# Graph attention with layer norm on one core: the mean for rows without neighbours moved from a VectorE pass into the bias of ScalarE's copy of the outputs

## The reference, cut to what matters

```python
def _L0_gnn_ref(feat_in, adj, W, b, w_src, w_dst, H_w, H_b):
    h = jnp.einsum('bnd,ade->bane', feat_in, W)
    th = jnp.tanh(h)
    attn_src = jnp.einsum('bane,aeo->bano', th, w_src)
    attn_dst = jnp.einsum('bane,aeo->bano', th, w_dst)
    attn = attn_src + jnp.swapaxes(attn_dst, 2, 3)
    attn = jnp.where(attn >= 0, attn, LEAKY_ALPHA * attn)
    mask = ~adj[:, None, :, :]
    attn = jnp.where(mask, jnp.float32(-999.0), attn)
    attn = jax.nn.softmax(attn, axis=-1)
    feat_out = jnp.einsum('banm,bame->bane', attn, h) + b
    feat_out = jnp.swapaxes(feat_out, 1, 2).reshape(feat_in.shape[0], feat_in.shape[1], -1)
    feat_out = jax.nn.elu(feat_out)
    gate = jax.nn.sigmoid(feat_in @ H_w.T + H_b)
    return gate * feat_out + (1.0 - gate) * feat_in
x = _layernorm(x + _L0_gnn_ref(...), axis=-1)
```

## Time and profile before

| | |
|---|---|
| median of 3 runs | 711.69 us (711.6 to 712.4) |
| the profiled execution | 711.58 us, span 709.8 us from first to last instruction |
| busy, share of the span | PE 96%, DVE 96%, POOL 85%, ACT 58% |
| granted TensorE clock, mean | 0.990 of full speed |
| length of one of steps 2 to 13 | 42.0 us |
| busy in 340.00 to 382.00 us | PE 41.46, DVE 41.02, POOL 38.38, ACT 25.56 |

### The profile page before, as it was taken

One profiled execution on the slowest core, in us unless ns is written; L12 is line 12 of the kernel. 1 busy time (PEld: TensorE's weight loads), 2 busy tenths in 40 slices (PEclk: granted clock), 3 DMA queues, 4 the chain that ended last, 5 costly groups with the idle time before them and its releaser, 6 DMA issues.

```text
span 709.8 us, 12409 instructions
## 1 busy us (share of the span) xinstructions
PE 678.0 (96%) x3327; PEld 376.1 (53%) x3327; DVE 678.3 (96%) x1225; ACT 412.4 (58%) x859; POOL 601.0 (85%) x434
## 2 busy tenths in 40 slices
PE   8899999999999999999999999999999999999882
PEld 5464655546555555555655554564646455554530
DVE  7699999999999999999999999999999999999996
ACT  5324558284664838567383765828476482855673
POOL 2964798998989899898989989899898989988393
PEclk9999999999999999999999999999999999999997
DMA  5253335263352615335261443426244351533402
GB/s 193 101 176 117 101 104 196 66 210 112 130 168 94 203 59 188 112 132 173 94 221 59 148 149 134 163 89 213 84 134 163 111 186 61 169 108 128 161 30 89
DMA packets 47083, 94.55 MB, mean 133 GB/s; under 512 B 2962, under 2 KB 28308, under 8 KB 47060
## 3 DMA queue, kind: packets, MB, share of 16 engines
q1 hardware_dynamic: 38868, 82.08, 35.5%
q10 hardware_dynamic: 8192, 12.19, 4.6%
HBM read 81.28 MB, written 12.98 MB: 133 GB/s over the span
## 4 chain that ended last, share of the span: by engine, by line
PE 72%; ACT 10%; DVE 7%; issue 5%; POOL 4%; DMA 2%; ACTq 0%; DVEq 0%; SPq 0%; POOLq 0%
PE out_T L976 37%; PE hg L898 28%; PE tr L984 4%; DVE ew L743 4%; ACT xT_hi L450 3%; ACT scratch L521 2%; ACT att_T L497 1%; PE hg L959 1%; ACT h_sb L462 1%; DMA xT_in<-in_xT 1%; DMA v_all<-v_rows 1%; DVE ex L778 1%; DVE att L761 1%; PE hg L931 1%; DVE att L772 1%
## 5 line engine op out<-in xcount | busy, mean ns | idle before, releaser
L743 DVE SCALAR_TENSOR_TENSOR ew<-v_all,u,adj 128x512 f32<-128x512 f32 x768 | 526.0, 732 | 0.5 <-DMA v_all<-v_rows 0.5
L976 PE MATMUL out_T<-ew,vals 128*64 128x512 f32 x1536 | 367.6, 602 | 2.7 <-DVE ew L743 2.7
L976 PEld LDWEIGHTS out_T<-ew,vals 128*64 128x64 f32 x1536 | 107.3, 137 | 198.3 <-issue 154.7
L301 POOL TENSOR_TENSOR th_w<-th,score_w 128x768 f32<-128x768 f32 x58 | 107.6, 1855 | 48.0 <-ACT th L458 40.8
L497 ACT ACTIVATE att_T<-out_T,tiny 128x512 f32<-128x512 f32 x96 | 65.8, 685 | 134.7 <-PE out_T L976 134.7
L898 PE MATMUL hg<-w_hi,xT_hi 128*128 128x384 f32 x384 | 99.4, 367 | 8.9 <-ACT h_sb L462 6.5
L898 PEld LDWEIGHTS hg<-w_hi,xT_hi 128*128 128x128 f32 x384 | 61.8, 191 | 50.6 <-issue 47.3
L898 PE MATMUL hg<-w_lo,xT_hi 128*128 128x384 f32 x384 | 88.6, 338 | 0.0
L898 PE MATMUL hg<-w_hi,xT_lo 128*128 128x384 f32 x384 | 87.6, 335 | 0.0
L305 POOL TENSOR_TENSOR th_w<-th_w 128x384 f32<-128x384 f32 x58 | 78.1, 1347 | 4.5
L468 ACT ACTIVATE gate_tanh<-hg 128x384 f32<-128x384 f32 x64 | 31.2, 490 | 78.3 <-PE hg L898 78.3
(11 more groups left out here) (106 smaller groups left out, 734.5 us busy)
## 6 DMA issues: line engine op xcount, KB each, us to landing
v_all<-v_rows SPq DMA_DIRECT2D x96, 512.0 KB, 3.8
xT_in<-in_xT SPq DMA_DIRECT2D x16, 768.0 KB, 4.6
x_in<-in_x SPq DMA_DIRECT2D x15, 768.0 KB, 4.5
out<-y ACTq DMA_DIRECT2D x15, 768.0 KB, 5.3
adj_in<-in_adjT SPq DMA_DIRECT2D x16, 256.0 KB, 4.9
xT_in<-in_x SPq DMA_DIRECT2D x1, 768.0 KB, 6.0
ew<-in_W SPq DMA_DIRECT2D x1, 576.0 KB, 4.2
gate<-in_HwT SPq DMA_DIRECT2D x1, 576.0 KB, 8.0
```

Of the source, the lines that this page charges most:

```text
L301: g.tensor_tensor(th_w[:, c % 2], th[:, c].unsqueeze(1).broadcast_to([P, 2, D]), score_w[:], ALU.mult).then_inc(S["thw_done"], 1)
L743: ve.scalar_tensor_tensor(out=ew[:, (2 * C * j + i) % SLOTS, :], in0=v_all[:, j % VSLOTS, k], scalar=u[:, q, c, h:h + 1], in1=ADJ[c][:], o ...
L976: te.matmul(OUT[VW * k:VW * k + VW, :], vals[:, q, c, h, :], ew[:, t % SLOTS, :], start=(c == 0), stop=(c == C - 1)).then_inc(S["ew_free"], 1)
```

## The change

The mean is added before the division. With `TINY` = 2^-90, `mean_w` holds TINY/512, so `means` gives TINY x mean; ScalarE copies it to the new tile `out_bias` (128 x 6, one column for each pair of heads, with TINY itself in the rows of the denominators), and `copy_out(b, j)` adds column j as its `bias`. A row without neighbours then has TINY x mean over TINY. For the other rows to stay exact, `vals` is lifted by 2^60.

- `means` is now three matmuls with `hb_tot` as weights and one column each, into columns 384 to 386 of `HG[1]`. It stands before `attend(b, 0)` in every step.
- `out_biases` on ScalarE: 4 activations of 32 partitions x 3 elements, right before `copy_out(b, 0)`, which waits for them.
- `exps` has one more activation of 128 x 48 and two more waits on ScalarE's own results.
- `alone`, `add_means`, `means_alone` and the additions in the last step are gone. In the last step `exp_late` of the middle columns moves before `copy_out(b, 5)`, and VectorE multiplies by the gate in two pieces.
- `features(b+1, 3)`, and `gates(b, 1)` in the last step, waited for `add_means`; they now wait for `out_biases`.

```diff
-TINY = 1.2e-38
+TINY = 2.0 ** -90
+LIFT = 2.0 ** 60
...
-        mean_ps = HG[1][:, 0:D]
+        mean_ps = HG[1][:, D:D + H // 4]
...
-                g.memset(mean_w[:], 1.0 / N).then_inc(S["pool_setup"], 1)
+                g.memset(mean_w[:], TINY / N).then_inc(S["pool_setup"], 1)
...
-                pool.wait_ge(S["exps_done"], NEX * b + 1)
+                pool.wait_ge(S["exps_done"], NEX * b + 2)
...
-                pool.wait_ge(S["att_done"], HP * b + 3)
-                pool.wait_ge(S["mean_last_done"], C)
-                g.tensor_tensor(att[:, q, :, EARLY], att[:, q, :, EARLY], mean_last[:, :, EARLY],
-                                ALU.add).then_inc(S["att_last_done"], 1)
...
-                a.activation(vals[:, q, :, :, E], d_rel[:], ACT.Exp, scale=ALPHA).then_inc(S["exps_done"], 1)
+                a.activation(s_pos[:], d_rel[:], ACT.Exp, scale=ALPHA).then_inc(S["exps_done"], 1)
+                act.wait_ge(S["exps_done"], NEX * b + 1)
+                a.activation(vals[:, q, :, :, E], s_pos[:], ACT.Copy, scale=LIFT).then_inc(S["exps_done"], 1)
...
+            def out_biases(b):
+                act.wait_ge(S["hm_done"], b + 1)
+                act.wait_ge(S["outT_copied"], HP * b)
+                m = out_bias[:].rearrange("p (i s) -> p i s", s=2)
+                for r in range(4):
+                    rows = slice(VW * (r % 2), VW * (r % 2) + E)
+                    a.activation(m[rows, :, r // 2], mean_ps[E * r:E * r + E, :], ACT.Copy).then_inc(S["out_bias_done"], 1)
...
-                a.activation(att_T[:, j % 2], OUT[:], ACT.Identity, bias=tiny[:, 0:1]).then_inc(S["outT_copied"], 1)
+                if j == 0:
+                    act.wait_ge(S["out_bias_done"], 4 * b + 4)
+                a.activation(att_T[:, j % 2], OUT[:], ACT.Identity, bias=out_bias[:, j:j + 1]).then_inc(S["outT_copied"], 1)
...
-                act.wait_ge(S["att1_done"], C * b + C)
+                act.wait_ge(S["att_done"], HP * b + HP)
...
+                out_biases(b)
                 copy_out(b, 0)
...
-                means_alone()
                 row_sums(b - 1)
                 copy_out(b, 3)
                 exp_early(q)
                 copy_out(b, 4)
                 row_squares(b - 1)
+                exp_late(q, 0, MIDDLE)
                 copy_out(b, 5)
...
-            def add_means(b, q):
-
-                dve.wait_ge(S["att_done"], HP * b + HP)
-                dve.wait_ge(S["hm_done"], b + 1)
-                dve.wait_ge(S["alone_done"], b + 1)
-                for c in range(C):
-                    ve.scalar_tensor_tensor(out=att[:, q, c], in0=mean_ps, scalar=alone[:, c:c + 1],
-                                            in1=att[:, q, c], op0=ALU.mult, op1=ALU.add).then_inc(S["att1_done"], 1)
...
-                dve.wait_ge(S["mean_last_done"], C)
-                add_means_late(MIDDLE, HP * B - 1)
+                dve.wait_ge(S["gate1_done"], B)
+                elu_late(0, MIDDLE)
                 dve.wait_ge(S["y_early_done"], 2)
                 statistics(0, EARLY)
                 inverses()
                 quotients()
-                add_means_late(FINAL, HP * B)
-                elu_late(0, MIDDLE)
+                gated(MIDDLE, 1)
                 elu_late(1, FINAL)
+                gated(FINAL, 2)
                 y = y_last[:, :, LATE]
-                dve.wait_ge(S["elu_late_done"], 2)
-                ve.tensor_tensor(y, y, gate[:, :, LATE], ALU.mult).then_inc(S["y_late_done"], 1)
...
-                    pe.wait_ge(S["att1_done"], C * (b - 1))
+                    pe.wait_ge(S["out_bias_done"], 4 * b)
...
-                    pe.wait_ge(S["att1_done"], C * b)
+                    pe.wait_ge(S["out_bias_done"], 4 * b + 4)
...
-                pe.wait_ge(S["gate_done"], C * b + C)
-                te.matmul(mean_ps, mean_w[:, 0:1].broadcast_to([P, P]), hb_tot[:, q], start=True, stop=True).then_inc(S["hm_done"], 1)
+                if isinstance(b, int) and b == 0:
+                    pe.wait_ge(S["hcopy_done"], C + 2)
+                else:
+                    pe.wait_ge(S["gate_done"], C * b)
+                for i in range(H // 4):
+                    last = te.matmul(mean_ps[:, i:i + 1], hb_tot[:, q, i * P:(i + 1) * P], mean_w[:, 0:1],
+                                     start=True, stop=True)
+                last.then_inc(S["hm_done"], 1)
```

More of the change, by code:

```diff
@@ L104, in gat_layernorm @@
         rden = sb("rden", [P, C, 2])
-        alone = sb("alone", [P, C])
         att = sb("att", [P, 2, C, D])
@@ L607, in x_last_form @@
                 a.activation(x_plus1[:], x_last, ACT.Identity, bias=plus1[:, 0:1]).then_inc(S["x_forms_done"], 1)
-            def means_alone():
-                act.wait_ge(S["hm_done"], B)
-                act.wait_ge(S["alone_done"], B)
-                for c in range(C):
-                    a.activation(mean_last[:, c], mean_ps, ACT.Copy, scale=alone[:, c:c + 1]).then_inc(S["mean_last_done"], 1)
             def exp_early(q):
                 y = y_last[:, :, EARLY]
-                act.wait_ge(S["att_last_done"], 1)
+                act.wait_ge(S["att_done"], HP * (B - 1) + 3)
                 act.wait_ge(S["mixed"], 3 * (B - 1) + 3)
@@ L751, in inverses @@
                     dve.wait_ge(S["tr_done"], HP * b + j + 1)
-                    if j == 0:
-                        if not isinstance(b, int) or b:
-                            dve.wait_ge(S["att1_done"], C * b)
-                        ve.tensor_scalar(alone[:], t[:, :, 0, E], TINY, None, ALU.is_le).then_inc(S["alone_done"], 1)
                     ve.reciprocal(rden[:], t[:, :, :, E]).then_inc(S["inv_done"], 1)
@@ L805, in step @@
                     edges(b, q, j, between)
-                    if j == 0 and not first:
-                        add_means(b - 1, 1 - q)
             def after():
@@ L825, in statistics, with gated @@
                         ve.bn_stats(stats[:, c, k], y_last[:, c, cols]).then_inc(S["stats_done"], 1)
-                dve.wait_ge(S["mean_last_done"], C)
-                add_means_late(MIDDLE, HP * B - 1)
+                def gated(cols, count):
+                    dve.wait_ge(S["elu_late_done"], count)
+                    ve.tensor_tensor(y_last[:, :, cols], y_last[:, :, cols], gate[:, :, cols], ALU.mult).then_inc(S["y_late_done"], 1)
+                dve.wait_ge(S["gate1_done"], B)
+                elu_late(0, MIDDLE)
                 dve.wait_ge(S["y_early_done"], 2)
@@ L991, in step_last @@
                 gates(b, q, 0, True)
+                means(b, q)
                 attend(b, q, 0)
@@ L1001, in step_last @@
                 attend(b, q, 2)
-                means(b, q)
                 transpose_out(b, 2)
```

28 lines of the change are left out of this document (12 added, 16 removed).

## The result

The changed kernel takes 728.1 us (median of 4 runs, 726.6 to 728.3) where the kernel before, on the same chip, takes 712.05: the ratio of the means is 1.0219, with a 95% interval from 1.0201 to 1.0237. It is slower by 16.1 us. I had forecast 722.6, so sign and mechanism came out as forecast and the size did not; the median also lies 0.1 us above the upper end that I gave, 728.0. The profiled execution has a span of 726.3 us against 709.8.

The account below looks back on a forecast made before the run. A circle through ScalarE, POOL and VectorE was taken to set the 42.0 us step. Terms 2.8 + 0.5 + 7.2 + 1.85 - 1.35 = +11.0 us on 711.58 gave 722.6 us, range 714 to 728.

Parts of the forecast that it names:

- What bounds the kernel: Middle steps: a closed circle of waits without idle time, not TensorE, sets 42.0 us; relieving VectorE gains nothing.
- The circle through ScalarE, POOL and VectorE: POOL's shift, ScalarE's normalising to tanh of chunk 2, POOL's weigh(2), VectorE's elu, POOL's weigh(3) to next shift: 42.0 us.
- Rival 1: Middle steps: VectorE's relief pays and TensorE sets the step, -0.4 us each, 709.7 us in all; chance 0.10.
- The four activations: ScalarE, before each step's first output copy: they add 0.55 us a step, bounds 0.4 and 1.3.
- the circle's term: Steps 2 to 14: the small activations' 0.55 us in each of 13 steps, +7.2 us.
- Rival 3: ScalarE's small activations run one after another at full length, 1.3 us a step, 733 us in all; chance 0.06.
- Rival 2: ScalarE's small activations are hidden by overlap or won back; the step stays 42.0 us, 715.4 us in all; chance 0.08.
- TensorE's means: Before TensorE's first product: 0.5 us a step, hidden in middle steps, counted once in step 1 as +0.5 us.
- The start: Step 0: TensorE's first product waits for ScalarE's copy of chunk 1, then runs at low clock; +2.8 us (+0.6 to +3.4).
- The last step: Step 15: gates(15, 1) waits for out_biases, delaying the transposes and second product; +1.85 us (1.6 to 2.6).
- The end: After the last quotients: less work remains, saving 1.2 us, and the quotients come 0.15 sooner; -1.35 us.

## Why the prediction was right, and where its sizes failed

**What bounds the kernel: right.** The circle through ScalarE, POOL and VectorE, read from four timelines side by side, held in each test: taking 2.1 us from VectorE, busy 96%, gave nothing, and 0.72 us on ScalarE, busy 58%, cost 0.82 a step. In the nine profiles in which the elu keeps its old place, it ends 1.60 to 1.63 us after POOL's instruction L301 (L300 or L302 in the other kernels) in each middle step, though it is issued anywhere from 0.6 to 1.6 us into it.

**Rival 1 (the relief pays): refuted** in the place where the change puts it. Its deciding point was the right one, though: the elu has to be issued before POOL's instruction. The move of the elu makes that happen, and then the relief pays 5.5 us.

**The four activations: the term that was mis-sized.** I took 0.09 us from start to start, from the read of an accumulator that follows its own activation. Measured are 0.19 us for each of four in a row: they are 0.16 us long and do not overlap, where I had let them overlap by half. So the sum of 0.55 had to be 0.75. Half the length of the 48-element activation, 0.15, would have come nearer than the row that looked more alike. With 0.75 the circle's term is 9.8 of the 10.6 measured. Over the middle steps the mean is 0.78 us more between `x_forms` and the copy, and 0.06 more ahead of the tanh, whose cause is open. Rival 3, 1.3 us a step, is refuted. The Trainium skill's figure of about 0.3 us for an ACTIVATE ("ScalarE: Activation LUTs", "Rules for kernel authors"), by which the prediction put the four at 1.2 us a step, is given there for one whose bias is a [128,1] operand, plus 0.83 ns an element. The copy of an output is such a one, and its 0.69 us for 512 elements agree with it (0.3 + 0.43). The four small ones have no such operand, so the figure was not theirs.

**Rival 2 (the activations are hidden): refuted**, but its number was wrong as well. With the activations gone the step is 42.3 and not 42.0. I had compared TensorE's own work without its wait, 41.6 us, with the circle, and so missed the second circle, which runs through TensorE and the same elu. In the changed kernel TensorE's means are hidden, as I said: the first product ends at 381.25, and the copy starts at 381.81.

**The start: right in kind, too small.** Of +4.75 us, 1.36 are not the price of the means. TensorE's first features took 1.20, 1.17 and 1.17 us per three matmuls where the kernel before has 0.76, 0.68 and 0.68, with a granted clock of 0.59 from 7 to 11 us and the same instructions there as in the kernel before, whose clock was 1.00. The kernel without the activations has the means in the same place and a clock of 1.00 there, and its first copy starts at 38.69:

```profile
31.80 1.41 PE L934 MATMUL hg<-mean_w,hb_tot 128*128 128x1 f32 x6 [4.11 <-ACT h_sb L457]
33.14 5.41 PE L958 MATMUL out_T<-ew,vals 128*64 128x512 f32 x16
...
38.69 0.69 ACT L498 ACTIVATE att_T<-out_T,out_bias 128x512 f32<-128x512 f32 x1 [7.03 <-PE out_T L958]
```

That is +3.4, the price of the change, and 0.6 over my 2.8: the means began at 31.80 and not 31.6, and took 1.34 us from start to start at 1.2 GHz and not 1.0; the product took 5.41 us for 5.4. Of the 1.36 us, 1.16 are there when the means begin (32.96 against 31.80); the other 0.2 lie in the product, and I put them down to the clock as well without having shown it.

**TensorE's means** took 0.65 us in place of 0.5 and cost +0.54 in step 0, forecast 0.5. **The last step**, +1.81 for +1.85, went by the rows in kind, since TensorE's gate products waited 1.52 us for the biases. That it fits to 0.04 is partly luck: counted from the first copy of step 14 they came 2.14 us later, and 0.33 of that was made up ahead of the reciprocals. **The end**, -1.23 for -1.35: from the last quotients to the last addition it is 1.91 us where it was 2.91, so 1.0 saved and not 1.2, and the quotients came 0.23 sooner and not 0.15. Two slips of arithmetic in the prediction changed nothing: 664.82 + 0.5 is 665.32 and 1.88 after 663.44, and the lower figure of Rival 1 is 704.9 by its own terms, not 706.5.

In sum 11.0 us were forecast and 16.5 measured: of the 5.5 that were missing, 3.4 come from the circle, most of it the size of a small activation, 1.4 from the start's low clock, and 0.6 from the start's own cost. My bounds for the activations went up to 1.3 us a step, but the range ended at 0.8 without a reason given; that holds what was measured, 0.82, nearly. It had no room for a start that is slower for another reason. The timed runs of the changed kernel, 726.6 once at a mean granted clock of 0.989 and 728.1 to 728.3 three times at 0.987, would fit one without and three with that low clock; this is argued, not shown.

## What to carry to other kernels

Before an engine is relieved, find out whether its work lies in the circle that sets the step, by following one step through all timelines until it closes; the busy shares pointed here at VectorE, whose relief was worth nothing. A relief and the order that lets it count belong together: alone each of them gave 0 and 6 us, together 12. Small instructions that are put ahead of the one for which everybody waits are paid in each step; between two conversions elsewhere in the same queue they were free.

## What the runs showed of the hardware that I had not expected

- Four activations of 32x3 elements in a row take 0.72 us when they read PSUM (162 ns mean) and 0.87 when they read SBUF (200 ns mean). They start 0.19 and 0.22 us apart, so they do not overlap, while the tanh and the copy of 128x384 elements, 0.49 us long, start 0.37 to 0.39 apart.
- Three one-column matmuls in float32 leave six records and take 0.65 us at 2.4 GHz and 1.34 at 1.2 GHz. Their six loads of 128x128 weights keep PEld busy for 0.81 us in step 8 of the changed kernel.
- VectorE's elu and POOL's L301 exclude each other whichever comes first. The elu first: it takes 1.75 us, and L301 2.83 instead of 1.86. L301 first: the elu takes 1.87 to 2.87 us in the middle steps of the kernels run here, the longer the earlier it is issued, and the POOL instruction behind L301 2.40 instead of 1.0.
- The granted clock from 7 to 11 us was 0.59 in the profile of the changed kernel and 1.00 in that of the kernel before, at the same instructions. Five of the twelve profiles have 0.59 to 0.67 there and seven 1.00; the kernel before with only the elu moved is one of the five, the changed kernel without activations one of the seven. No edit touches the instructions there, and it costs some 1.2 us by the time the means begin. Whether the execution decides it or the program is open.
- In the kernel before, the first product took 5.96 us with the clock at 0.50 for 3.3 us of it; with the clock at 1.00 throughout it took 5.59. It waits for VectorE's edge tiles, so the low clock there cost little.
